# Convolution and attention kernel on one Trainium2 core: row maxima spread over the attention block, and two of its sixteen subtractions per block moved to GpSimd

## The chip, the core and the metric

The kernel runs on one core of a Trainium2 chip. Its engines are TensorE (PE, with its weight loads shown as PEld), VectorE (DVE), ScalarE (ACT), GpSimd (POOL) and SyncE (SP, which only issues transfers here). Each runs its own list of instructions in order and waits on counting semaphores. The metric is the device time of one execution in microseconds, lower is better.

## The reference, cut to what matters

```python
# x: (8, 192, 64, 64).  Layer 0: attention inside each image, 4096 positions, 192 channels
xn = _gn(x)                                   # group norm, 32 groups
q  = prelu(conv1x1(xn, w1, b1), a1)           # 24 channels
k  = prelu(conv1x1(xn, w2, b2), a2)           # 24 channels
v  = prelu(conv1x1(xn, wa, ba), aa)           # 192 channels
score = softmax(einsum('bnc,bcm->bnm', q, k), axis=2)
x  = x + einsum('bnm,bmc->bnc', score, v)     # transposed back to (b, c, h, w)
# Layer 1: a per-channel chain of small (1, 3, 3, 3, 1) maps with tanh gates, at x-0.5 and x+0.5
lower, upper = logits(_gn(x) - 0.5), logits(_gn(x) + 0.5)
s = -sign(lower + upper)
x = x + maximum(abs(sigmoid(s * upper) - sigmoid(s * lower)), 1e-6)
```

## The kernel before

The eight images are worked one after another. For each there is a `phase_a` (projections q, k, v of this image, interleaved with layer 1 of the image before) and a `phase_b` (the attention). This change touches `phase_b` alone.

`phase_b` has 8 **blocks** j of 512 query columns. A block has 16 **pairs** p, each of two times 128 keys. For a pair, PE makes the scores (`scores`, 2 products of 512 columns, L1261) two pairs ahead; ACT takes the exponential twice, once to fp16 (`e_hi`, L732) and once to fp32 (`e_32`, L735, semaphore `full_ready`); DVE makes the **lower part** `e_lo = e_32 - e_hi` (`low`, L1058, 128x1024, semaphore `lo_ready`); and PE multiplies both halves with v in 8 groups of 3 products (L1486, L1488, L1490) into the block's own two PSUM banks. `e_32` has two buffers, so ACT's fp32 pass of pair q waits for the lower part of pair q-2.

The softmax needs the row maxima of the *next* block before its scores. In block j PE therefore also makes 32 **max tiles** for block j+1 (`max_tile`, L1438, one product of 128x512 each) in the two free PSUM banks, and DVE reduces each to one column (`reduce`, L1164, semaphore `max_red`). Tile m waits until reduction m-2 is done. `max_tiles(p, first)` says which tiles belong to pair p: in block 0 four per pair from pair 3, in the others three per pair from pair 0; `spots` says after which of the 8 groups they stand. After the last one DVE runs `split_max` (6 small steps, L1006 to L1011), PE transposes the result (`turn_max`, L1240, before pair 12), DVE copies it out (`rows_out`, L1018) and SP carries it into `qst`.

At a block's start DVE takes the reciprocal of the row sums of the block before (`denominators`, L1025), ACT scales its output (`normalise`, 4 passes, L722, semaphore `out_norm`), POOL splits it (`split_out`, L688 and L690), PE turns it back in two halves (`turn_parts`, L1253, at the ends of pairs 12 and 13) and DVE adds x and takes statistics (`add_half`, L1033 and L1035). The free banks are those of the block before, so the first max tiles wait for `out_norm`.

Beside this run the **tails** of layer 1 of the image before: two units per block in blocks 0 to 5, and none during image 0. A unit is `sums` and `difference` on POOL (L582, L588, L593), `halves` and `size` on ACT, `result` on DVE (L1053, in pairs 7 and 15). ACT's `halves` stand in pairs 2 and 9, and POOL's L588 waits for them. DVE's order inside a pair p is: (p = 0: `denominators`), `low` of pair p+1, the reductions of pair p, then `result`.

Of the kernel before, what the change touches and what calls it, by code (L numbers as in the profile page):

```python
# [5 lines left out]
ALU = mybir.AluOpType  # L6
# [18 lines left out]
LN2 = 0.6931471805599453  # L25
ESHIFT = 14 * LN2
BIG = 4096.0
PER_STEP = 3
START = 1


# [82 lines left out]
    return USES[n - 1] if n == len(USES) - 1 else USES[n - 3] if n >= 3 else None  # L114


def max_tiles(p, first):

    per, begin = (4, 3) if first else (PER_STEP, 0)
    return list(range(max(per * (p - begin), 0), min(max(per * (p - begin + 1), 0), MAXES)))  # L120


def tail_unit(i, last):
# [26 lines left out]
def program(nc, x, wall, cols, g6, sel, eye, diag, mraw, fraw, braw, x2d, out):  # L150
    x_rows = x.rearrange("b c h w -> (b c) (h w)")
    out_rows = out.rearrange("b c h w -> (b c) (h w)")
    with ExitStack() as ctx:
# [348 lines left out]
        def _(pool):  # L502
# [155 lines left out]
            def moments(b, which):  # L658
# [17 lines left out]
                else:  # L676
                    step(pool.tensor_scalar(mv_next[:, :, 0], minus_mean1[:, :], -1.0, None, ALU.mult))
                    step(pool.tensor_scalar(mv_next[:, :, 1], total1[:, :], 1.0 / HW, None, ALU.mult))

            def split_out(b, j):  # L680

                normalised = pool.compute_val(b * BLOCKS + j + 1 + START)
                turned = pool.compute_val(b * 2 * BLOCKS + 2 * j + START)
                cast = pool.compute_val(b * (BLOCKS - 1) + j + 1)
                settle(pool)
                pool.wait_ge(out_norm, normalised)
                pool.wait_ge(out_turn, turned)
                pool.tensor_copy(o_parts[:, 0, :, :], o_sb[:, :, :]).then_inc(out_hi, 1)  # L688
                pool.wait_ge(out_hi, cast)
                pool.tensor_tensor(o_parts[:, 1, :, :], o_sb[:, :, :], o_parts[:, 0, :, :], ALU.subtract  # L690
                                   ).then_inc(out_split, 1)

            def phase_b(b, l):
                for j in range(BLOCKS):
                    if j == 4:
                        moments(b, 0)
                    if j == BLOCKS - 1:
                        moments(b, 1)
                    if j >= 1:
                        split_out(b, j - 1)  # L700
                    if l is not None:
                        for i in tails_in(j, HALVES_AT).values():
                            sums(l, i, False)
                            difference(l, i, False)
                root1(pool.compute_val(b + 1))

            root1(None)
# [9 lines left out]
        def _(act):  # L717
# [9 lines left out]
            def exps(pairs, q):  # L727
                sc = ps[:, 2 * (q % 2):2 * (q % 2) + 2, :]
                act.wait_ge(scored, pairs + (q + 1))
                if q >= 4:  # L730
                    act.wait_ge(summed, pairs + (q - 3))
                act.activation(e_hi[:, q % 4, :].rearrange("p (k n) -> p k n", k=2), sc, ACT.Exp)  # L732
                if q >= 2:
                    act.wait_ge(lo_ready, pairs + (q - 1))
                act.activation(e_32[:, q % 2, :].rearrange("p (k n) -> p k n", k=2), sc,  # L735
                               ACT.Exp).then_inc(full_ready, 1)

# [89 lines left out]
            def phase_b(b, l):  # L827
# [21 lines left out]
                for j in range(BLOCKS):  # L849
                    pairs = act.compute_val(b * BLOCKS * PAIRS)  # L850
                    for p in range(PAIRS):
                        if p == 0 and j > 0:
                            normalise(b, j - 1)
                        if p + 2 < PAIRS or j + 1 < BLOCKS:
                            exps(pairs, j * PAIRS + p + 2)
# [18 lines left out]
        def _(dve):  # L874
# [286 lines left out]
            def phase_b(b, l):  # L1161
                def reduce(base, m, bank):
                    dve.wait_ge(max_mm, base + (m + 1))
                    dve.tensor_reduce(mxp[:, m // BLOCKS, m % BLOCKS:m % BLOCKS + 1], ps[:, bank + m % 2, :],  # L1164
                                      AX_X, ALU.max).then_inc(max_red, 1)

                for j in range(BLOCKS):
# [6 lines left out]
                    for p in range(PAIRS):  # L1174
                        if p == 0 and not first:
                            denominators(b, j - 1)
                        if p == 12 and not last:
                            rows_out(nxt, free, False)
                        if p + 1 < PAIRS or not last:
                            low(pairs, p + 1)  # L1180
                        if first and l is not None and p == 1:
                            logits(l, UNITS - 1, False)
                        if not last:
                            for m in max_tiles(p, first):
                                reduce(maxes, m, free)
                            if p == 11:
                                split_max(nxt, maxes)
                        if not first and p in (13, 14):
                            add_half(b, j - 1, p - 13)
                        if l is not None and p in tails_in(j, RESULT_AT):  # L1190
                            result(l, tails_in(j, RESULT_AT)[p], False)
                        if last and p == 2:
# [17 lines left out]
        def _(pe):  # L1210
# [220 lines left out]

            def phase_b(b, l):
                def max_tile(base, q_col, m, bank, evacuated):
                    if m >= 2:
                        pe.wait_ge(max_red, base + (m - 1))
                    elif evacuated is not None:
                        pe.wait_ge(out_norm, evacuated + START)
                    pe.matmul(ps[:, bank + m % 2, :], qst[:, q_col + m // BLOCKS * P:q_col + (m // BLOCKS + 1) * P],  # L1438
                              kst[:, (m % BLOCKS) * N:(m % BLOCKS + 1) * N], start=True, stop=True
                              ).then_inc(max_mm, 1)  # L1440

                for j in range(BLOCKS):
# [6 lines left out]
                    for p in range(PAIRS):  # L1449
                        if p == 12 and not last:  # L1450
                            turn_max(blocks + 1, free)
                        if p + 2 < PAIRS or not last:
# [4 lines left out]
                        pe.wait_ge(lo_ready, pairs + (p + 1))  # L1457
# [38 lines left out]
                        if not first and p in (12, 13):  # L1496
                            if p == 12:
                                pe.wait_ge(out_split, b * (BLOCKS - 1) + j)
                            elif not last:
                                pe.wait_ge(max_rows, blocks + 2)  # L1500
                            turn_parts(j - 1, p - 12)

                pe.wait_ge(full_ready, pairs + PAIRS)
                project(0)
# [71 lines left out]
```

## Time and profile before

| | |
|---|---|
| median of 3 runs | 4865.89 us (4865.57 to 4873.28) |
| profiled execution | 4868.1 us, its span 4866.3 us |
| granted TensorE clock, mean of the span | 0.982 |
| busy share | PE 92%, DVE 86%, ACT 76%, POOL 19% |
| chain that ended last | PE 57%, DVE 17%, issue 13%, ACT 12% |
| reductions of max tiles in `phase_b` (L1164) | 1792, mean 683 ns |
| lower parts (L1058) | 1024, mean 1316 ns |

A row of the timeline gives start, duration, engine, line, operation, what is written from what, and how many instructions were merged in the row; in brackets how long the engine sat idle before it, and who ended that. Successive instructions of an engine overlap a little, so the distance from start to start is shorter than the duration. A busy share is an average over phases with different limits.

### The profile page before, as it was taken

What the parts mean: (1) busy time and instruction counts of PE and PEld (TensorE: products, weight loads), DVE (VectorE), ACT (ScalarE), POOL (GpSimd) and SP (SyncE); (2) the same over time, 40 slices, a digit from 0 to 9 for tenths busy, and PEclk for the clock granted to TensorE, in tenths of its full rate; (3) what the DMA queues carried; (4) which work ended last, traced back from release to release, by engine and by line L of the source; (5) the groups of instructions that cost most, each with busy time, mean ns of one, the idle gap of its engine ahead of it and who ended that gap; (6) DMA issues with size and microseconds to landing.
All of it is one profiled execution on the core that took longest, in us unless ns stands there. A gap on an engine that the chain in (4) does not pass through costs nothing.

```text
span 4866.3 us, 107519 instructions
## 1 busy us (share of the span) xinstructions
PE 4460.5 (92%) x38780; PEld 2978.2 (61%) x38780; DVE 4178.8 (86%) x5433; ACT 3717.8 (76%) x4214; POOL 937.5 (19%) x937
## 2 busy tenths in 40 slices
PE   6999989999899998999899998999989999899976
PEld 4888347773477725777257762678617785277821
DVE  6897899978999798996999969899698987989866
ACT  2776887768877697776977769777797777977787
POOL 4200202212122111221112120121202212022112
PEclk9999999999999999999999999999999999999988
DMA  2001421114211142111412023120332113311133
GB/s 66 25 20 30 100 70 47 34 39 105 62 47 40 36 110 51 47 40 46 108 45 57 28 62 98 39 58 27 77 86 60 36 38 73 96 42 34 38 88 95
DMA packets 154989, 279.95 MB, mean 58 GB/s; under 512 B 37441, under 2 KB 37921, under 8 KB 152706
## 3 DMA queue, kind: packets, MB, share of 16 engines
q1 hardware_dynamic: 154434, 272.69, 21.8%
q8 instruction: 331, 5.42, 0.5%
q14 instruction: 224, 1.84, 0.1%
HBM read 205.24 MB, written 50.33 MB: 53 GB/s over the span
## 4 chain that ended last, share of the span: by engine, by line
PE 57%; DVE 17%; issue 13%; ACT 12%; DMA 1%; DVEq 0%; ACTq 0%; SPq 0%; POOL 0%; POOLq 0%
PE ps L1486 10%; PE ps L1488 10%; PE ps L1490 10%; PE ps L1261 7%; DVE mxp L1164 6%; PE ps L1438 6%; ACT th L777 5%; ACT arena L770 5%; DVE arena L1058 4%; PE ps L1360 3%; PE ps L1294 3%; DVE th L1096 3%; PE ps L1346 3%; PE ps L1318 2%; PE ps L1253 1%
## 5 line engine op out<-in xcount | busy, mean ns | idle before, releaser
L1486 PE MATMUL ps<-v_sb,arena 128*128 128x193 f16 x8192 | 2017.5, 246 | 18.4 <-DVE arena L1058 18.4
L1488 PE MATMUL ps<-v_sb,arena 128*128 128x192 f16 x8192 | 2026.6, 247 | 0.0
L1490 PE MATMUL ps<-v_sb,arena 128*128 128x193 f16 x8192 | 2009.6, 245 | 0.0
L732 ACT ACTIVATE arena<-ps 128x1024 f16<-128x1024 f32 x1024 | 1049.9, 1025 | 773.8 <-PE ps L1261 772.8
L1058 DVE TENSOR_TENSOR arena<-arena 128x1024 f16<-128x1024 f32 x1024 | 1346.1, 1316 | 258.4 <-ACT arena L735 258.3
L1164 DVE TENSOR_REDUCE mxp<-ps 128x1 f32<-128x512 f32 x1792 | 1162.2, 683 | 32.5 <-PE ps L1438 24.8
L1096 DVE SCALAR_TENSOR_TENSOR th<-th,gates,ps 128x1024 f32<-128x1024 f32 x768 | 949.9, 1275 | 148.7 <-ACT th L777 141.4
L735 ACT ACTIVATE arena<-ps 128x1024 f32<-128x1024 f32 x1024 | 1046.4, 1022 | 0.2 <-DVE arena L1058 0.2
L1488 PEld LDWEIGHTS ps<-v_sb,arena 128*128 128x128 f16 x8192 | 794.8, 97 | 261.8 <-issue 0.3
L777 ACT ACTIVATE th<-ps,biases 128x1024 f32<-128x1024 f32 x768 | 826.1, 1120 | 119.9 <-PE ps L1346 81.5
L1486 PEld LDWEIGHTS ps<-v_sb,arena 128*128 128x128 f16 x8192 | 792.0, 97 | 150.5 <-issue 28.6
L1490 PEld LDWEIGHTS ps<-v_sb,arena 128*128 128x128 f16 x8192 | 807.2, 99 | 0.2
L1438 PE MATMUL ps<-kst,qst 128*128 128x512 f16 x1792 | 680.3, 380 | 56.1 <-DVE mxp L1164 49.7
L1261 PE MATMUL ps<-qst,kst 128*128 128x512 f16 x2048 | 612.5, 381 | 12.3 <-DMA qst<-mrows 8.5
L1360 PE MATMUL ps<-th,w 64*64 64x512 f32 x3072 | 421.4, 617 | 112.1 <-DVE th L1096 107.6
L770 ACT ACTIVATE arena<-x,biases,scl 128x1024 f32<-128x1024 f32 (+1 forms) x400 | 499.6, 1249 | 16.2 <-DVE biases L986 15.5
L1346 PE MATMUL ps<-arena,w1s 64*64 64x512 f32 x3072 | 426.6, 624 | 39.3 <-DMA arena<-x2d 8.3
L1346 PEld LDWEIGHTS ps<-arena,w1s 64*64 64x64 f32 x3072 | 90.8, 133 | 313.0 <-issue 292.6
L1360 PEld LDWEIGHTS ps<-th,w 64*64 64x64 f32 x3072 | 95.7, 133 | 280.0 <-issue 279.8
L1438 PEld LDWEIGHTS ps<-kst,qst 128*128 128x128 f16 x1792 | 172.4, 96 | 112.0 <-DVE mxp L1164 103.9
L1261 PEld LDWEIGHTS ps<-qst,kst 128*128 128x128 f16 x2048 | 184.7, 97 | 88.3 <-DMA qst<-mrows 14.9
L758 ACT ACTIVATE lu<-ps 128x384 f32<-128x384 f32 (+1 forms) x192 | 102.8, 536 | 170.6 <-PE ps L1269 117.1
(147 smaller groups left out, 3448.3 us busy)
## 6 DMA issues: line engine op xcount, KB each, us to landing
x<-x2d SPq DMA_DIRECT2D x1152, 64.0 KB, 2.4
arena<-x2d SPq DMA_DIRECT2D x768, 64.0 KB, 2.5
xp<-x_dram SPq DMA_DIRECT2D x18, 1536.0 KB, 10.1
shared<-x_dram SPq DMA_DIRECT2D x64, 384.0 KB, 3.7
x2d<-shared SPq DMA_DIRECT2D x64, 384.0 KB, 3.0
res<-x2d SPq DMA_DIRECT2D x96, 256.0 KB
out_dram<-res SPq DMA_DIRECT2D x96, 256.0 KB
kst<-shared SPq DMA_DIRECT2D x32, 256.0 KB, 3.3
```

The costliest lines, as they stand in the source:

```text
L732: act.activation(e_hi[:, q % 4, :].rearrange("p (k n) -> p k n", k=2), sc, ACT.Exp)
L735: act.activation(e_32[:, q % 2, :].rearrange("p (k n) -> p k n", k=2), sc, ACT.Exp).then_inc(full_ready, 1)
L770: ins = act.activation(t0[lo:hi, v % T0R, d, :], x4[lo:hi, v % X4R, :], ACT.Tanh, bias=biases[lo:hi, d, 0, u:u + 1], scale=scl[lo:hi, u:u ...
L777: act.activation(dst, ps[:, at:at + 2, :], ACT.Tanh, bias=biases[:, d, layer, u:u + 1]).then_inc(after, 1)
L1058: dve.tensor_tensor(e_lo[:, q % 4, :], e_32[:, q % 2, :], e_hi[:, q % 4, :], ALU.subtract).then_inc(lo_ready, 1)
L1096: dve.scalar_tensor_tensor(t, t, gates[:, c // 4, col:col + 1], ps[:, at:at + 2, :], ALU.mult, ALU.add).then_inc(after, 1)
L1164: dve.tensor_reduce(mxp[:, m // BLOCKS, m % BLOCKS:m % BLOCKS + 1], ps[:, bank + m % 2, :], AX_X, ALU.max).then_inc(max_red, 1)
L1261: ins = pe.matmul(ps[:, 2 * (q % 2) + i, :], kst[:, m * P:(m + 1) * P], qst[:, q_col:q_col + N], start=True, stop=True)
L1438: pe.matmul(ps[:, bank + m % 2, :], qst[:, q_col + m // BLOCKS * P:q_col + (m // BLOCKS + 1) * P], kst[:, (m % BLOCKS) * N:(m % BLOCKS + 1 ...
L1486: pe.matmul(acc, eh, v_sb[:, m, 0:C + 1], start=(m == 0 and t % 2 == 0), stop=False, skip_group_check=True)
L1488: pe.matmul(acc[:, 0:C], eh, v_sb[:, m, VW:VW + C], start=False, stop=False, skip_group_check=True)
L1490: ins = pe.matmul(acc, el, v_sb[:, m, 0:C + 1], start=False, stop=(m == MT - 1), skip_group_check=True)
```

## The change

The 32 max tiles of a block are laid out anew. Five of them (tiles 0 to 4) are made, and reduced, one block earlier, in its pairs 13, 14 and 15 (`EARLY_AT`: one, two and two tiles), where blocks 1 to 7 had none; the other 27 stand in pairs 0 to 10 as 2, 3, 2, 3, ... (`PER_PAIR`). The early ones exist for the maxima of blocks 2 to 7 (`j + 2 < BLOCKS`, so they are made in blocks 0 to 5). The two banks of the tiles swap. Because early tiles are in the banks in which the next block adds up, PE waits at pair 0 for `max_red` to reach the fifth of them; the wait for `out_norm` now stands before tiles 5 and 6. `turn_parts` and `add_half` move up one pair. In blocks 0 to 6 the lower parts of pairs 7 and 8 are made by POOL, counted on `lo_pool`, and POOL's `sums` and `difference` of the block's second unit come behind them.

```diff
+POOL_LOWS = (7, 8)
+EARLY_AT = {13: [0], 14: [1, 2], 15: [3, 4]}
+EARLY = 5
+PER_PAIR = [2, 3, 2, 3, 2, 3, 2, 3, 2, 3, 2]
...
 def max_tiles(p, first):
-    per, begin = (4, 3) if first else (PER_STEP, 0)
-    return list(range(max(per * (p - begin), 0), min(max(per * (p - begin + 1), 0), MAXES)))
+    if first:
+        return list(range(max(4 * (p - 3), 0), min(max(4 * (p - 2), 0), MAXES)))
+    begin = EARLY + sum(PER_PAIR[:p])
+    return list(range(begin, begin + PER_PAIR[p])) if p < len(PER_PAIR) else []
...
+def early_tiles(j, p):
+    return EARLY_AT.get(p, []) if j + 2 < BLOCKS else []
...  # GpSimd
+            def low(b, q):
+                full = pool.compute_val(b * BLOCKS * PAIRS + q + 1)
+                settle(pool)
+                pool.wait_ge(full_ready, full)
+                pool.tensor_tensor(e_lo[:, q % 4, :], e_32[:, q % 2, :], e_hi[:, q % 4, :], ALU.subtract
+                                   ).then_inc(lo_pool, 1)
...  # ScalarE, exps
                 if q >= 2:
-                    act.wait_ge(lo_ready, pairs + (q - 1))
+                    made, count = lower_part(b, q - 2)
+                    act.wait_ge(made, count)
...  # VectorE
-                        if p + 1 < PAIRS or not last:
+                        if (p + 1 < PAIRS or not last) and not by_pool(j * PAIRS + p + 1):
                             low(pairs, p + 1)
...
-                        if not first and p in (13, 14):
-                            add_half(b, j - 1, p - 13)
+                        if not first and p in (12, 13):
+                            add_half(b, j - 1, p - 12)
+                        for m in early_tiles(j, p):
+                            reduce(dve.compute_val(maxes + MAXES), m, free)
...  # TensorE
                     if m >= 2:
                         pe.wait_ge(max_red, base + (m - 1))
-                    elif evacuated is not None:
+                    if evacuated is not None and m in (EARLY, EARLY + 1):
                         pe.wait_ge(out_norm, evacuated + START)
...
                         if p == 0 and not first:
                             pe.wait_ge(x2_ready, b * 2 * BLOCKS + 2 * (j - 1) + START)
+                            if not last:
+                                pe.wait_ge(max_red, maxes + EARLY)
...
-                        spots = (1, 3, 5, 7) if first else (5, 6, 7) if p == 0 else (2, 5, 7)
+                        spots = (1, 3, 5, 7) if first else (5, 7) if p == 0 else (2, 5, 7) if len(todo) == 3 else (3, 7)
+                        ahead = early_tiles(j, p).copy()
...
+                                if i * NT + t in ((6,) if p == 13 else (4, 7)) and ahead:
+                                    if ahead[0] < 2 and first:
+                                        pe.wait_ge(max_rows, blocks + 2)
+                                    elif ahead[0] < 2:
+                                        pe.wait_ge(x2_ready, b * 2 * BLOCKS + 2 * (j - 1) + ahead[0] + 1 + START)
+                                    max_tile(pe.compute_val(maxes + MAXES), q_next + N, ahead.pop(0), free, None)
```

On DVE, at the end of pair 15 of a block and the start of the next, before (`low`, the unit's `result`, and the reciprocal that opens the next block, then `low` and the first reductions):

```order
L1058 TENSOR_TENSOR arena<-arena 128x1024
L1053 SCALAR_TENSOR_TENSOR res<-lu,res 128x512
L1169 ISA
L1025 RECIPROCAL rden<-ps 128x4
L1057 REGISTER_ALU
L1058 TENSOR_TENSOR arena<-arena 128x1024
```

and now, at the same place:

```order
L1099 TENSOR_TENSOR arena<-arena 128x1024
L1204 REGISTER_ALU
L1205 TENSOR_REDUCE mxp<-ps 128x1
L1204 REGISTER_ALU
L1205 TENSOR_REDUCE mxp<-ps 128x1
L1094 SCALAR_TENSOR_TENSOR res<-lu,res 128x512
L1210 ISA
L1066 RECIPROCAL rden<-ps 128x4
L1098 REGISTER_ALU
L1099 TENSOR_TENSOR arena<-arena 128x1024
```

Two early reductions now stand between the lower part and the `result`, and so also ahead of the reciprocal.

On POOL, one block with two units, before (`split_out`, then `sums` and `difference` of both units):

```order
L688 CAST o_parts<-o_sb 128x768
L690 TENSOR_TENSOR o_parts<-o_sb,o_parts 128x768
L582 TENSOR_TENSOR lu_sign<-lu 128x512
L588 TENSOR_TENSOR lu<-lu 128x512
L593 TENSOR_TENSOR lu<-lu,lu_sign 128x512
L582 TENSOR_TENSOR lu_sign<-lu 128x512
L588 TENSOR_TENSOR lu<-lu 128x512
L593 TENSOR_TENSOR lu<-lu,lu_sign 128x512
```

and now:

```order
L722 CAST o_parts<-o_sb 128x768
L724 TENSOR_TENSOR o_parts<-o_sb,o_parts 128x768
L609 TENSOR_TENSOR lu_sign<-lu 128x512
L615 TENSOR_TENSOR lu<-lu 128x512
L620 TENSOR_TENSOR lu<-lu,lu_sign 128x512
L708 REGISTER_ALU
L711 TENSOR_TENSOR arena<-arena 128x1024
L708 REGISTER_ALU
L711 TENSOR_TENSOR arena<-arena 128x1024
L609 TENSOR_TENSOR lu_sign<-lu 128x512
L615 TENSOR_TENSOR lu<-lu 128x512
L620 TENSOR_TENSOR lu<-lu,lu_sign 128x512
```

The two lower parts (L711) stand between the two units.

On PE, at the end of pair 11, before (the last group, the transpose of the maxima, the scores of pair 14):

```order
L1486 MATMUL ps<-v_sb,arena 128x193
L1488 MATMUL ps<-v_sb,arena 128x192
L1490 MATMUL ps<-v_sb,arena 128x193
L1240 MATMUL ps<-eye,mparts 12x128
L1261 MATMUL ps<-qst,kst 128x512 x2
```

and now:

```order
L1534 MATMUL ps<-v_sb,arena 128x193
L1536 MATMUL ps<-v_sb,arena 128x192
L1538 MATMUL ps<-v_sb,arena 128x193
L1296 MATMUL ps<-eye,o_parts 96x128 x8
L1283 MATMUL ps<-eye,mparts 12x128
L1304 MATMUL ps<-qst,kst 128x512 x2
```

The first `turn_parts` (L1296) has come ahead of the transpose of the maxima (L1283).

## Rows read from the trace of the kernel before

**Rows 1.** The page's first line.

```profile
span 4866.3 us, 107519 instructions
```

**Rows 2.** The view of waits: engine, tile, line <- releaser: us, times, longest us.

```profile
PE ps L1438 <- DVE mxp L1164: 49.7, 141, 0.8
```

**Rows 3.** Timeline of DVE, image 2, block 3 with two units.

```profile
1427.07 0.18 DVE L1025 RECIPROCAL rden<-ps 128x4 f32<-128x4 f32 x1 [0.64 <-PE ps L1490]
...
1429.22 1.89 DVE L1164 TENSOR_REDUCE mxp<-ps 128x1 f32<-128x512 f32 x3 [0.55 <-PE ps L1438]
1431.02 1.44 DVE L1058 TENSOR_TENSOR arena<-arena 128x1024 f16<-128x1024 f32 x1
1432.39 1.87 DVE L1164 TENSOR_REDUCE mxp<-ps 128x1 f32<-128x512 f32 x3
...
1437.25 2.05 DVE L1058 TENSOR_TENSOR arena<-arena 128x1024 f16<-128x1024 f32 x1
1439.21 1.87 DVE L1164 TENSOR_REDUCE mxp<-ps 128x1 f32<-128x512 f32 x3
...
1463.61 1.21 DVE L1058 TENSOR_TENSOR arena<-arena 128x1024 f16<-128x1024 f32 x1
1464.74 0.17 DVE L1006 TENSOR_REDUCE mx<-mxp 128x4 f32<-128x32 f32 x1
...
1475.64 0.68 DVE L1053 SCALAR_TENSOR_TENSOR res<-lu,res 128x512 f32<-128x512 f32 x1
1476.97 0.18 DVE L1025 RECIPROCAL rden<-ps 128x4 f32<-128x4 f32 x1 [0.65 <-PE ps L1490]
```

**Rows 4.** Timeline of ACT, the same block.

```profile
1427.36 1.36 ACT L722 ACTIVATE o_sb<-ps,rden 128x192 f32<-128x192 f32 x4
1428.59 1.04 ACT L732 ACTIVATE arena<-ps 128x1024 f16<-128x1024 f32 x1
...
1433.98 1.02 ACT L732 ACTIVATE arena<-ps 128x1024 f16<-128x1024 f32 x1 [1.22 <-PE ps L1261]
```

**Rows 5.** Timeline of POOL, the same block.

```profile
1429.74 1.64 POOL L690 TENSOR_TENSOR o_parts<-o_sb,o_parts 128x768 f16<-128x768 f32 x1
...
1436.94 1.27 POOL L588 TENSOR_TENSOR lu<-lu 128x512 f32<-128x512 f32 x1 [3.35 <-ACT lu L742]
1438.38 2.03 POOL L593 TENSOR_TENSOR lu<-lu,lu_sign 128x512 f32<-128x512 f32 x1 [0.17 <-POOL lu L588]
```

**Rows 6.** Timeline of PE, the same block.

```profile
1426.78 0.25 PE L1490 MATMUL ps<-v_sb,arena 128*128 128x193 f16 x1
1426.87 0.59 PE L1261 MATMUL ps<-qst,kst 128*128 128x512 f16 x2
1427.30 0.25 PE L1486 MATMUL ps<-v_sb,arena 128*128 128x193 f16 x1
...
1428.80 0.38 PE L1438 MATMUL ps<-kst,qst 128*128 128x512 f16 x1
...
1439.95 0.39 PE L1438 MATMUL ps<-kst,qst 128*128 128x512 f16 x1 [0.48 <-DVE mxp L1164]
1440.17 0.59 PE L1261 MATMUL ps<-qst,kst 128*128 128x512 f16 x2
...
1465.97 0.22 PE L1240 MATMUL ps<-eye,mparts 128*12 128x128 f16 x1 [0.87 <-DVE mparts L1011]
...
1468.57 0.61 PE L1253 MATMUL ps<-eye,o_parts 128*96 128x128 f16 x8
```

**Rows 7.** Timelines of POOL and DVE where both start almost together.

```profile
156.15 1.01 POOL L565 TENSOR_TENSOR w<-th 128x192 f32<-128x192 f32 x2
...
156.66 1.58 DVE L1058 TENSOR_TENSOR arena<-arena 128x1024 f16<-128x1024 f32 x1
...
694.11 2.35 POOL L582 TENSOR_TENSOR lu_sign<-xp 128x512 f32<-128x512 f32 x1
694.12 1.22 DVE L1058 TENSOR_TENSOR arena<-arena 128x1024 f16<-128x1024 f32 x1
```

More of the change, by code:

```diff
@@ L27 @@
 BIG = 4096.0
-PER_STEP = 3
+POOL_LOWS = (7, 8)
+EARLY_AT = {13: [0], 14: [1, 2], 15: [3, 4]}
+EARLY = 5
+PER_PAIR = [2, 3, 2, 3, 2, 3, 2, 3, 2, 3, 2]
 START = 1
@@ L114, in tile_user, with by_pool, lows_of @@
     return USES[n - 1] if n == len(USES) - 1 else USES[n - 3] if n >= 3 else None
+def by_pool(q):
+    return q // PAIRS + 1 < BLOCKS and q % PAIRS in POOL_LOWS
+def lows_of(pool, n):
+    return sum(by_pool(q) == pool for q in range(n))
 def max_tiles(p, first):
-    per, begin = (4, 3) if first else (PER_STEP, 0)
-    return list(range(max(per * (p - begin), 0), min(max(per * (p - begin + 1), 0), MAXES)))
+    if first:
[4 more added lines that the diff above has]
+    return EARLY_AT.get(p, []) if j + 2 < BLOCKS else []
 def tail_unit(i, last):
@@ L296, in program @@
         lo_ready = sem("lo_ready")
+        lo_pool = sem("lo_pool")
         summed = sem("summed")
@@ L330, in settle, with lower_part @@
             eng.wait_ge(consts_in, CONST_DMAS * 16)
+        def lower_part(b, q):
+            pool = by_pool(q)
+            return lo_pool if pool else lo_ready, b * lows_of(pool, BLOCKS * PAIRS) + lows_of(pool, q + 1)
         def counter(l):
@@ L700, in phase_b @@
                         split_out(b, j - 1)
[L701 to L704, printed above, removed]
+                    now = tails_in(j, HALVES_AT) if l is not None else {}
+                    for q in POOL_LOWS:
+                        if q == POOL_LOWS[0] and HALVES_AT[0] in now:
+                            sums(l, now[HALVES_AT[0]], False)
+                            difference(l, now[HALVES_AT[0]], False)
+                        if by_pool(j * PAIRS + q):
+                            low(b, j * PAIRS + q)
+                    if HALVES_AT[1] in now:
+                        sums(l, now[HALVES_AT[1]], False)
+                        difference(l, now[HALVES_AT[1]], False)
                 root1(pool.compute_val(b + 1))
@@ L725, in normalise, with exps @@
                 ins.then_inc(out_norm, 1)
-            def exps(pairs, q):
+            def exps(pairs, q, b=None):
                 sc = ps[:, 2 * (q % 2):2 * (q % 2) + 2, :]
@@ L854, in phase_b @@
                         if p + 2 < PAIRS or j + 1 < BLOCKS:
-                            exps(pairs, j * PAIRS + p + 2)
+                            exps(pairs, j * PAIRS + p + 2, b)
                         if l is not None:
@@ L1163, in reduce @@
                     dve.wait_ge(max_mm, base + (m + 1))
-                    dve.tensor_reduce(mxp[:, m // BLOCKS, m % BLOCKS:m % BLOCKS + 1], ps[:, bank + m % 2, :],
+                    dve.tensor_reduce(mxp[:, m // BLOCKS, m % BLOCKS:m % BLOCKS + 1], ps[:, bank + (m + 1) % 2, :],
                                       AX_X, ALU.max).then_inc(max_red, 1)
@@ L1435, in max_tile @@
                         pe.wait_ge(max_red, base + (m - 1))
-                    elif evacuated is not None:
+                    if evacuated is not None and m in (EARLY, EARLY + 1):
                         pe.wait_ge(out_norm, evacuated + START)
-                    pe.matmul(ps[:, bank + m % 2, :], qst[:, q_col + m // BLOCKS * P:q_col + (m // BLOCKS + 1) * P],
+                    pe.matmul(ps[:, bank + (m + 1) % 2, :], qst[:, q_col + m // BLOCKS * P:q_col + (m // BLOCKS + 1) * P],
                               kst[:, (m % BLOCKS) * N:(m % BLOCKS + 1) * N], start=True, stop=True
@@ L1456, in phase_b @@
                             scores(q_col if p + 2 < PAIRS else q_next, p + 2)
-                        pe.wait_ge(lo_ready, pairs + (p + 1))
+                        made, count = lower_part(b, j * PAIRS + p)
+                        pe.wait_ge(made, count)
                         if p == 0 and first:
@@ L1495, in phase_b @@
                                     max_tile(maxes, q_next, todo.pop(0), free, None if first else blocks)
-                        if not first and p in (12, 13):
-                            if p == 12:
+                                if i * NT + t in ((6,) if p == 13 else (4, 7)) and ahead:
[4 more added lines that the diff above has]
+                                    max_tile(pe.compute_val(maxes + MAXES), q_next + N, ahead.pop(0), free, None)
+                        assert not todo and not ahead
+                        if not first and p in (11, 12):
+                            if p == 11:
                                 pe.wait_ge(out_split, b * (BLOCKS - 1) + j)
+                                if not last:
+                                    pe.wait_ge(max_red, maxes + MAXES)
                             elif not last:
                                 pe.wait_ge(max_rows, blocks + 2)
-                            turn_parts(j - 1, p - 12)
+                            turn_parts(j - 1, p - 11)
                 pe.wait_ge(full_ready, pairs + PAIRS)
```

## The prediction

> **What bounds the kernel now.** I read the page first: PE 92% and DVE 86% of the span [rows 1] say only that two engines are close. Then the view of waits: PE stands for a reduction of a max tile 141 times [rows 2]; its weight loads wait likewise. So where PE waits inside the attention, it is for DVE's reductions, which stand behind `low` in DVE's list. Then the timelines of one block with two units: from reciprocal to reciprocal it takes 1476.97 - 1427.07 = 49.90 us [rows 3]. There are 35 such blocks (blocks 1 to 5 of seven images).
>
> PE's own work in it, from starts to starts [rows 6]: 18 products in 1428.80 - 1427.30 = 1.50, so 24 in 2.00 and a group of three in 0.25; the scores 0.44; a max tile 0.22 (512 columns; 0.215 below); a `turn_parts` 0.61 less the 0.17 by which an end outlasts its start, 0.44; `turn_max` 0.15. Sum: 16 x 2.44 + 32 x 0.215 + 0.88 + 0.15 = 46.9. **So PE stands 3.0 us per such block.** DVE's list is nearly as long: a lower part is followed after 1.13 (1463.61 to 1464.74), a reduction after 0.60 (three in 1.80) [rows 3].
>
> The 3.0 us, part by part: pair 0, 0.23 (its third tile needs the first reduction: 1428.80 + 0.42 + 0.68 + 0.06 = 1429.96 against 1429.73). Pair 1, 0.08 (first reduction at 1432.39). Before pair 12, 1.04 (0.87 idle for `split_max` [rows 6], and the 0.17 of the product's tail). The rest, 1.6 us, is DVE's backlog: in pairs 3 and 4 POOL's tail collides with `low` (2.05 instead of 1.21 [rows 3, 5]), 0.48 of one wait is seen before the tile at 1439.95 [rows 6], and in pair 8 it is the `result` of 0.60.
>
> **What the change does.** PE's products are the same in number. I replay one block with units; zero is the start of the last product of pair 15 (1426.78), every offset from the rows.
>
> *Moved: the early tiles.* The fifth follows that product at 0.08; its reduction starts 0.42 later (1428.80 to 1429.22 [rows 3, 6]), at 0.50, and is done at 1.18. Pair 0 would start at 0.52 + 0.22 = 0.74; the new wait holds it to 1.24 (0.06 from reduction to PE: 1439.21 + 0.68 to 1439.95). **Stall (a) 0.50**, before 0.
>
> *Added: what is queued behind that reduction.* On DVE the `result` (1.10, 0.60 long) and the reciprocal, now at 1.70 and not at 0.29. ACT's `normalise` starts 0.29 later, at 2.0, and lasts 1.36 [rows 3, 4]: `out_norm` at 3.36, where tile 5 is due at 1.24 + 1.50 = 2.74 and gets in at 3.43. **Stall (b) 0.69**, before 0.23. Without a unit the reciprocal is at 1.10, and (b) is 0.07.
>
> *What is late next.* Pair 1 starts at 3.43 + 0.22 + 0.50 + 0.22 + 0.44 = 4.81. POOL's L690 starts 2.38 after `normalise` (1429.74 - 1427.36), at 4.38, and ends at 6.02; ACT's first pass for pair 2 starts 1.23 after it, at 3.23, so its lower part is due at about 5.2 and finds POOL in its way. DVE is free for reductions 1.01 after L690's end (1431.38 to 1432.39 [rows 3, 5]), at 7.03; tile 7 is reduced at 7.71, tile 9 enters at 7.77 and was due at 4.81 + 2.43 = 7.24. **Stall (c) 0.53**, before 0.08; without a unit it is 0.55, by the same steps.
>
> *Pairs 3 and 4.* L588 starts 2.96 after ACT's pass for pair 4, and `low` 0.31 after L588 (1437.25 - 1436.94): blocked. Pair 2 now has two tiles, so `low` comes one tile, 0.22, sooner: 0.09 after L588. Who wins? A `low` 0.01 behind POOL's start took its plain 1.22 and POOL 2.35 (plain 1.27); where it was about 0.03 behind the second of two L565, it took 1.58 and ended 1.08 after them [rows 7]. So POOL wins from some 0.03 on, and 0.09 is on its side by 0.06 only. Then DVE is free 2.27 after L588's start (1439.21 - 1436.94); L588 starts 3.15 into pair 2 (the pass at 1433.98 starts 0.63 after its scores, these 0.44 before the pair; estimate from the 0.59 of the scores [rows 6]), the tile two after it enters at 3.15 + 2.27 + 0.68 + 0.06 = 6.16 and was due at 2.87 + 2.43 = 5.30. **Stall (d) 0.86**, before 1.2 (the rest above less pair 8); the fewer tiles after it hold no second one.
>
> The Trainium skill, "SBUF — State Buffer", section "SBUF: two separate sides", says that a DVE operation with two SBUF inputs and a GpSimd operation exclude each other for a whole instruction, and that the one that starts first gets the ports. The long rows agree (2.05, 2.35); the 0.01 case went to the later one. By the rule as by my threshold (d) stays; it speaks against giving POOL more such work.
>
> *Removed from DVE: two lower parts*, 2 x 1.13 = 2.3 us per block. They empty DVE in pairs 6 to 8 and cover the `result` of pair 7: **stall in pair 8 gone, 0.4**. Elsewhere PE does not wait for DVE's total, so the rest buys nothing. POOL's lower part is not in the trace: L690 is the same subtraction with 768 columns, 1.64, so 1.64 x 1024/768 = 2.19; bounds 1.64, and 2.19 + 1.08 = 3.3 when it must first let a `low` pass (694.11: 2.35 - 1.27). It is due some 4 us after `full_ready` (scores two pairs ahead, 5.9 before their products, less 0.6 and two passes of 1.0, gives 3.7 to 4.0), so it is hidden at either bound. ACT's pass of pair 9 waits for pair 7's later still. The unit behind them is needed by ACT in pair 9 and is ready in pair 8.
>
> *Moved: `turn_parts`* now fills the wait for `split_max`. The collision at `low` of pair 11 stays (three tiles in pair 9, as now): free at 5.42 of pair 9, two reductions, `low` at 6.62, `turn_max` 2.36 later (1463.61 to 1465.97) at 8.98; PE is ready at 3.08 + 2.87 + 2.00 + 0.44 = 8.39. **Stall (e) 0.59**, before 1.04. Without units: `low` 3.23 into pair 10, `turn_max` at 5.59, PE ready at 5.31, 0.28 against 0.22, since the last tile now stands later in its pair.
>
> **Sum.** With units: 0.50 + 0.69 + 0.53 + 0.86 + 0.59 = 3.17 against 3.0: +0.17 x 35 = +6. Image 0, blocks 1 to 5: 0.50 + 0.07 + 0.55 + 0.28 = 1.40 against 0.23 + 0.08 + 0.22 = 0.53: +0.87 x 5 = +4.4. Block 0 (8 of them): five tiles more on PE +1.08, stall (a) at its end +0.50, and in pairs 6 and 7, where four reductions and a `low` (4 x 0.62 + 1.13 = 3.6) outlast PE's 3.30, -0.64: +0.94 x 8 = +7.5. Block 6: five tiles fewer, -1.08, new stalls 1.50 (b, c, 0.28) or 0.90 in image 0, old ones 0.53: -0.11 x 7 - 0.7 = -1.5. Block 7 and `phase_a`: 0. Total +16 us. The profiled execution (4868.1) lies 2.2 above the median; I apply the sum to the median: **4882 us**.
>
> **Rivals.** (1) *DVE wins in pair 3.* It needs `low` 0.06 earlier or L588 later; then (d) is gone, the block takes 49.2, and the sum is 16 - 0.86 x 35 = -14: 4852. For it: the small margin; against: both offsets repeat from block to block. (2) *The boundary stalls do not come*, because the early reductions are done before PE asks. Then the block falls to PE's own 46.9 and (e), 47.5: 2.4 x 35 = 84 less, block 0 +4: 4786. For it: DVE loses 2.3 us of work; against: the fifth tile is PE's last product before the wait. (3) *POOL's pair is later than I think*: if the two lower parts together come 1.0 later, the unit behind them (L582, 1.27) meets DVE's `low` of pair 9 and holds PE some 0.9 in 42 blocks: +38, 4920. Below that point nothing. (4) *Part of each*: the stalls hide behind one another and the sum stays within 0.2%, about what a measurement of this kernel can tell: 4866.
>
> **How the numbers follow.** Forecast 0.50, (1) 0.16, (2) 0.08, (3) 0.09, (4) 0.17. The forecast's own range is 4873 to 4896 (0.2 us per block in blocks 1 to 6 is 8 us). Leaving out (2) and the far half of (3) the range is 4848 to 4905. Faster by over 0.2% has (1) and (2), 0.24; within 0.2% has (4) and a tail of the forecast, 0.21; slower has the rest, 0.55.
>
> **What would show it.** PE's first product of a block waiting for a reduction (some 48 times 0.5), tile 5 waiting for ACT's `normalise` 42 times 0.7, the reciprocal at 1.7 us after the block's last product, `low` of pair 4 at 2.2 us and no stall in pair 8, POOL's L711 at about 2.2 us. Wrong it would be if `low` of pair 4 takes 1.2 us, if L711 takes over 3.5, or if pair 0 starts without a wait.

## The result, and the profile after

| | before | after |
|---|---|---|
| median | 4867.85 us, 4 runs (4865.57 to 4873.28) | 4914.1 us, 4 runs (4911.66 to 4914.45) |
| ratio | 1 | 1.0091, 95% interval 1.0078 to 1.0104 |
| span of the profiled execution | 4866.3 us | 4912.6 us |

One execution of all that are told of here, one of e9, took 5893 us at a granted clock of 0.725 (the others have 0.97 to 0.99) and enters no figure. The change makes the kernel slower, by 46 us where 16 were forecast: the time lies above the range. The page of the changed kernel, its first line and the engines, and from its list of groups (busy us, mean ns | idle before, releaser) three rows:

```profile
span 4912.6 us, 109567 instructions
...
PE 4461.2 (91%) x38780; PEld 2978.7 (61%) x38780; DVE 4078.4 (83%) x5321; ACT 3709.6 (76%) x4214; POOL 1161.4 (24%) x1049
...
L1534 PE MATMUL ps<-v_sb,arena 128*128 128x193 f16 x8192 | 2020.1, 247 | 61.5 <-POOL arena L711 25.5
...
L1205 DVE TENSOR_REDUCE mxp<-ps 128x1 f32<-128x512 f32 x1792 | 1196.8, 686 | 314.3 <-PE ps L1482 304.7
L1099 DVE TENSOR_TENSOR arena<-arena 128x1024 f16<-128x1024 f32 x912 | 1212.2, 1331 | 151.3 <-ACT arena L776 149.5
```

Against [rows 1] the span is 46.3 longer, and DVE is busy for less of it, 83% and not 86%: it lost 112 lower parts, and the kernel gained none of that time. The first group has the news: the products stood 25.5 us for POOL's L711. The view of one line says how often:

```profile
L711 POOL TENSOR_TENSOR arena<-arena x112: 2124/2127/2137, 146.7 to 4622.9; 128x1024 f16<-128x1024 f32 x112
...
  PE ps L1534: 25.5, 1
  ACT arena L776: 24.4, 1
```

Of 112 lower parts by POOL (2.13 us each, estimate 2.19) one pair held everybody, once, for 25.5 us. The first of them starts at 146.7. This is the timeline of POOL, and of PE, in block 0 of image 0:

```profile
98.05 1.26 POOL L551 TENSOR_TENSOR th<-th 128x12 f32<-128x12 f32 x1 [17.69 <-DVE th L951]
...
142.55 0.22 POOL L589 TENSOR_TENSOR th<-th 128x12 f32<-128x12 f32 x1
142.85 3.91 POOL L592 TENSOR_TENSOR w<-th 128x192 f32<-128x192 f32 x8
146.71 4.21 POOL L711 TENSOR_TENSOR arena<-arena 128x1024 f16<-128x1024 f32 x2
```

```profile
122.83 0.59 PE L1304 MATMUL ps<-qst,kst 128*128 128x512 f16 x2
148.89 0.34 PE L1534 MATMUL ps<-v_sb,arena 128*128 128x193 f16 x1 [25.47 <-POOL arena L711]
```

POOL is still working through its set-up: over a hundred steps on 12 columns, each waiting for the one before, from 98 to 143 us, and eight of 128x192 behind them, to 147. Before the change nobody wanted POOL in that block. Now PE asks for the lower part of pair 7 at 123 and gets it at 148.9. The clock fell while PE stood: granted 1.00 over 123 to 124, 0.90 over 124 to 126, 0.50 (1.2 GHz) over 126 to 151, and 1.00 again from 153. So the first products after the gap start 0.16 apart where they start 0.08 apart at the full clock; by an estimate, half of the 4 us from 149 to 153, that is 2 us more.

The length of each block, from the start of its first product to that of the next block's, read from the rows of PE for all 56:

| | before | after | forecast of the difference | difference |
|---|---|---|---|---|
| image 0, block 0 | 51.36 | 80.49 | +0.94 | +29.1 |
| images 1 to 7, block 0 (mean) | 52.67 | 53.85 | +0.94 | +1.18 |
| images 1 to 7, blocks 1 to 5 | 49.92 | 50.24 | +0.17 | +0.32 |
| image 0, blocks 1 to 5 (no units; mean) | 47.60 | 48.32 | +0.87 | +0.73 |
| block 6, images 1 to 7 | 47.52 | 47.38 | -0.11 | -0.14 |

Image 0's block 6, not in the table, went from 47.52 to 46.61, forecast -0.7. One block of 56 gives 29.1 of the 46.3. The view of waits of PE in the changed kernel, which answers to [rows 2]:

```profile
PE ps L1482 <- DVE mxp L1205: 53.4, 114, 0.8
...
PE ps L1482 <- ACT o_sb L762: 20.2, 42, 0.5
...
PE ps L1534 <- DVE mxp L1205: 17.6, 48, 0.4
```

The two lower rows are new, and they are the forecast's stalls (b), 42 times, and (a), 48 times (an idle row is 0.17 shorter than the delay, since an instruction's end outlasts the next one's start). The timelines of DVE and POOL in image 2, block 3, beside [rows 3, 5]:

```profile
1464.20 0.68 DVE L1094 SCALAR_TENSOR_TENSOR res<-x,res 128x512 f32<-128x512 f32 x1
1464.80 0.18 DVE L1066 RECIPROCAL rden<-ps 128x4 f32<-128x4 f32 x1
...
1474.76 2.26 DVE L1099 TENSOR_TENSOR arena<-arena 128x1024 f16<-128x1024 f32 x1
...
1490.62 0.68 DVE L1094 SCALAR_TENSOR_TENSOR res<-lu,res 128x512 f32<-128x512 f32 x1
1491.22 1.22 DVE L1099 TENSOR_TENSOR arena<-arena 128x1024 f16<-128x1024 f32 x1
```

```profile
1474.67 1.27 POOL L615 TENSOR_TENSOR lu<-lu 128x512 f32<-128x512 f32 x1 [3.35 <-ACT lu L783]
```

The block's first product starts at 1464.34 and the reciprocal that opens it only at 1464.80, behind the `result`; the lower part of pair 4 comes 0.09 after POOL's L615 and takes 2.26 instead of 1.21. Both are as the prediction has them.

### The profile page after: what moved, and what is told of

It reads as the page before. It is cut to its first block, busy times and chain, and to the rows that moved or that the text cites. A ratio compares the mean times of both kernels' runs of the same rounds, so it can differ in the third digit from the quotient of the medians.

```text
span 4912.6 us, 109567 instructions
## 1 busy us (share of the span) xinstructions
PE 4461.2 (91%) x38780; PEld 2978.7 (61%) x38780; DVE 4078.4 (83%) x5321; ACT 3709.6 (76%) x4214; POOL 1161.4 (24%) x1049
## 4 chain that ended last, share of the span: by engine, by line
PE 52%; DVE 16%; issue 14%; ACT 13%; DMA 1%; DVEq 1%; SPq 0%; ACTq 0%; POOL 0%; POOLq 0%
PE ps L1534 9%; PE ps L1536 9%; PE ps L1538 9%; PE ps L1304 6%; PE ps L1482 5%; DVE mxp L1205 5%; ACT th L818 5%; ACT arena L811 4%; DVE arena L1099 4%; PE ps L1403 4%; PE ps L1337 3%; PE ps L1389 3%; DVE th L1137 3%; PE ps L1361 2%; DVE res L1094 1%
## 5 line engine op out<-in xcount | busy, mean ns | idle before, releaser
L1534 PE MATMUL ps<-v_sb,arena 128*128 128x193 f16 x8192 | 2020.1, 247 | 61.5 <-POOL arena L711 25.5
L1205 DVE TENSOR_REDUCE mxp<-ps 128x1 f32<-128x512 f32 x1792 | 1196.8, 686 | 314.3 <-PE ps L1482 304.7
L1099 DVE TENSOR_TENSOR arena<-arena 128x1024 f16<-128x1024 f32 x912 | 1212.2, 1331 | 151.3 <-ACT arena L776 149.5
L711 POOL TENSOR_TENSOR arena<-arena 128x1024 f16<-128x1024 f32 x112 | 238.3, 2128 | 457.8 <-ACT arena L776 457.8
L722 POOL CAST o_parts<-o_sb 128x768 f16<-128x768 f32 x56 | 46.1, 823 | 912.0 <-ACT o_sb L762 881.7
```

Of the source, the lines that this page charges most:

```text
L1099: dve.tensor_tensor(e_lo[:, q % 4, :], e_32[:, q % 2, :], e_hi[:, q % 4, :], ALU.subtract).then_inc(lo_ready, 1)
L1534: pe.matmul(acc, eh, v_sb[:, m, 0:C + 1], start=(m == 0 and t % 2 == 0), stop=False, skip_group_check=True)
```

## The experiments

Line numbers of the experiments differ from those of the changed kernel by up to 6. Each ratio is against the kernel before as timed beside that run (medians 4867.99 us for e1 to e4, 4873.63 for e5 to e8, 4869.47 for e9 to e12), so between these three groups ratios compare and times do not quite. "Step of pair n" is from the first product of a pair to that of the next, as a mean over blocks 1 to 5 of images 1 to 7.

**e1_block0_by_dve**: the changed kernel, but in image 0, block 0, VectorE makes all lower parts.

```diff
-                        if by_pool(j * PAIRS + q):
+                        if by_pool(j * PAIRS + q) and not (l is None and j == 0):
...  # VectorE
+                        elif first and l is None and by_pool(p + 1):
+                            low(pairs, p + 1, lo_pool)
```

> The change, but in block 0 of image 0 the two lower parts stay with DVE, which counts them on lo_pool. Theory S (the part that was missed is GpSimd's set-up chain, behind which those two lower parts stood until 146.7 us; everything else is as the sum has it): block 0 of image 0 falls from 80.5 to about 52.3 us, the span from 4912.6 to about 4884.5, still some 17 us above the kernel before; no other block moves. Theory B (the lower part on GpSimd is late in general and block 0 is only where it shows first): other waits for GpSimd's lower part appear, and less than 15 of the 46 us come back, over 4897.

4886.44 us, ratio 1.0043 (1.0029 to 1.0057). Block 0 of image 0 takes 52.14 us; the other blocks are as in the changed kernel. So the 28 us are these two instructions' and no more. With them out the time stands 4 us from the forecast of 4882, which is closer than the sum deserves: in the profiled executions the 56 blocks together are 20.4 us longer than before, and what lies outside them 3.6 shorter.

**e2_lows_alone** and **e3_tiles_alone**: e1's kernel with the tiles, `turn_parts` and `add_half` of before, so that only POOL's lower parts are left of the change; and the changed kernel with all lower parts on VectorE, so that only the rest is.

```diff
-EARLY_AT = {13: [0], 14: [1, 2], 15: [3, 4]}
-EARLY = 5
-PER_PAIR = [2, 3, 2, 3, 2, 3, 2, 3, 2, 3, 2]
+EARLY_AT = {}
+EARLY = 0
+PER_PAIR = [3] * 10 + [2]
...  # e3
-POOL_LOWS = (7, 8)
+POOL_LOWS = ()
```

> The max tiles, turn_parts and add_half as in the kernel before; only the two lower parts per block on GpSimd (not in block 0 of image 0), with the second unit behind them. Theory R (PE waits only at single places, which the hand replay names): in blocks 1 to 5 of seven images the 0.43 before pair 9 and the 0.52 of pair 4 go (the second unit's L582 no longer meets the lower part of pair 5), the turn_max wait stays: 48.95 instead of 49.92; block 0 0.65 less. Sum -33 - 5 = -38, span 4828, ratio 0.992. Theory L (DVE's load bounds these blocks): 2.3 us in each of 56 blocks, down to PE's own time in most, -80 or more, under 4790.

> The tiles, turn_parts and add_half of the change; all lower parts on DVE, GpSimd's two units one behind the other as before. Theory R: nothing that GpSimd's lower parts bought is needed once the tiles are spread, but block 0 keeps its 0.65: span 4884.5 + 5 = 4890, blocks 1 to 5 50.2 as in the change. Theory L: 2.3 us more DVE work in each block costs time: blocks 1 to 5 over 51.5, span over 4930.

e2: 4855.33 us, 0.9976 (0.9966 to 0.9986), and not 4828. The change's lower parts alone, with POOL's second unit behind them, are worth 12 us: blocks 1 to 5 take 49.45 against 49.92, and all of it is at pair 4, whose step falls from 3.61 to 3.09 as the expectation has it. These are POOL and DVE of before there, and DVE of e2:

```profile
1440.55 1.27 POOL L582 TENSOR_TENSOR lu_sign<-lu 128x512 f32<-128x512 f32 x1
...
1441.01 1.89 DVE L1058 TENSOR_TENSOR arena<-arena 128x1024 f16<-128x1024 f32 x1
```

```profile
1439.51 1.21 DVE L1099 TENSOR_TENSOR arena<-arena 128x1024 f16<-128x1024 f32 x1
```

In e2 POOL starts that operation only after its two lower parts. So what the steps show is a collision put off, and not a relief of VectorE; the second unit put later without the lower parts was not tried. The stall of pair 8 did not go: its step stays at 3.51 against the 3.09 of its neighbours with three tiles. DVE's timeline there:

```profile
1450.49 1.41 DVE L1205 TENSOR_REDUCE mxp<-ps 128x1 f32<-128x512 f32 x2 [0.28 <-PE ps L1484]
1451.82 0.68 DVE L1094 SCALAR_TENSOR_TENSOR res<-lu,res 128x512 f32<-128x512 f32 x1
1452.41 1.22 DVE L1099 TENSOR_TENSOR arena<-arena 128x1024 f16<-128x1024 f32 x1
1453.55 1.88 DVE L1205 TENSOR_REDUCE mxp<-ps 128x1 f32<-128x512 f32 x3
```

DVE was idle just before (0.28), so it carries no backlog that fewer lower parts could empty; `result` and `low` stand back to back ahead of three reductions, and PE asks for the first while they run. Two tiles in pair 8 cure that (e3's step is 2.87), and so does a `result` that stands elsewhere (e12, below). e3: 4886.95 us, 1.0041 (1.0027 to 1.0055), within its interval of e1. **With the tiles of the change POOL's lower parts are worth nothing.**

**e4_result_earlier**: e1 with the second unit's `result` in pair 14, so that the reciprocal of the next block is behind one thing less.

```diff
-HALVES_AT, SIZE_AT, RESULT_AT = (2, 9), (5, 12), (7, 15)
+HALVES_AT, SIZE_AT, RESULT_AT = (2, 9), (5, 12), (7, 14)
```

> e1 with the second unit's result on DVE in pair 14 and not in pair 15, so that it no longer stands between the last early reduction and the reciprocal. Theory R: the wait for out_norm in pair 0 falls from 0.67 to 0.07 in 42 blocks, -26, span 4858. Rival (pair 0 and 1 wait for something else that comes at the same time, as GpSimd's split of the output): under 10 us come back, over 4874.

4864.63 us, 0.9998 (0.9988 to 1.0007): 22 us less than e1, where 26 were expected. The step of pair 0 falls from 3.54 to 2.93. Stall (b) was the `result` ahead of the reciprocal.

**e6_pair2_tile**: e4 with the second of pair 2's tiles one group of products earlier. It is to put VectorE's `low` of pair 4 ahead of POOL's L615; the number of tiles in each pair stays.

```diff
-... (2, 5, 7) if len(todo) == 3 else (3, 7)
+... (2, 5, 7) if len(todo) == 3 else (3, 6) if p == 2 else (3, 7)
```

> e4 with the second tile of pair 2 after the seventh group and not after the eighth, 0.25 us sooner, so that DVE asks for the lower part of pair 4 some 0.17 us before GpSimd starts L588 of the first unit. Theory R (who starts first has the ports): this lower part takes 1.2 instead of 2.26, wait (d) of 0.86 goes in 35 blocks, -30, span 4831, and GpSimd's L588 takes 2.3 instead of 1.27. Rival (DVE is short of time there anyway): the wait moves one pair on, under 10 us come back.

4837.15 us, 0.9928 (0.9911 to 0.9945). The step of pair 3 falls from 3.95 to 3.08, the block of image 2 from 49.61 to 48.75: stall (d), 0.86, is the collision. POOL and DVE of e6:

```profile
1438.48 2.18 POOL L615 TENSOR_TENSOR lu<-lu 128x512 f32<-128x512 f32 x1 [3.36 <-ACT lu L783]
...
1438.32 1.22 DVE L1099 TENSOR_TENSOR arena<-arena 128x1024 f16<-128x1024 f32 x1
```

`low` now starts 0.16 before POOL instead of 0.09 after, takes its plain 1.22, and it is POOL that takes 2.18.

**e5_four_early**: e4 with four early tiles and not five, the last of them after the fifth group of pair 15, and pair 6 with three instead; pairs 1 and 2 change places.

```diff
-EARLY_AT = {13: [0], 14: [1, 2], 15: [3, 4]}
-EARLY = 5
-PER_PAIR = [2, 3, 2, 3, 2, 3, 2, 3, 2, 3, 2]
+EARLY_AT = {13: [0], 14: [1, 2], 15: [3]}
+EARLY = 4
+PER_PAIR = [2, 2, 3, 3, 2, 3, 3, 3, 2, 3, 2]
```

> e4 with four early tiles instead of five, so that PE's last product of a block is no tile whose reduction it then waits for, and with two tiles in pair 1 and three in pairs 2 and 6. Theory R: wait (a) of 0.50 goes in 48 blocks (-24); the third tile of pair 1, whose wait (c) of 0.55 comes from GpSimd's split meeting the lower part of pair 2, is gone (-26); (d) in pair 3 is 0.65 instead of 0.86 (-7). Span 4861.3 - 57 = 4805. Rival (the waits at the boundary are GpSimd's split and ACT's scaling, whatever the tiles do): they move to the next pair, less than 25 come back, over 4836.

4814.84 us, 0.9883 (0.9866 to 0.9899). The step of pair 15 falls from 3.45 to 2.85, that of pair 1 from 3.63 to 2.86, and pair 3 has 3.73 instead of 3.95. Less the tile (0.215) that pairs 15 and 1 each lost, stall (c) is gone and stall (a) falls from 0.58 to 0.20. It was expected to go altogether. DVE and PE of e5 at the end of a block:

```profile
1418.38 0.69 DVE L1205 TENSOR_REDUCE mxp<-ps 128x1 f32<-128x512 f32 x1
...
1419.12 0.26 PE L1536 MATMUL ps<-v_sb,arena 128*128 128x193 f16 x1
```

The fourth tile's reduction stands behind a `low` and is done at 1419.07, 0.05 before the next block's first product starts. So the new wait of the change still bounds the block's start, by less.

**e11_five_without_pool**: e5 with every lower part on VectorE (`POOL_LOWS = ()`).

> This is e5_four_early with every lower part made by VectorE. It asks what the lower parts on GpSimd are worth once the tiles stand well. Theory A (nothing: VectorE has room around pairs 6 to 8, as e3_tiles_alone equals e1_block0_by_dve within its interval): 4815, within 8. Theory B (they carry the gain of e5: VectorE gets 2 lows of 1.13 us more in pairs 6 to 8, where it idles about 1.0 us): up to 1.3 us more in a block, 35 blocks, 4860.

4809.27 us, 0.988 (0.9864 to 0.9897): the same as e5. Blocks 1 to 5 take 48.50 against 48.56. VectorE's two lower parts more fall in pairs 6 to 8, where it idled between the reductions (in e5, 0.28, 0.71 and 0.28 us in a row).

**e9_two_tiles_in_pair2** and **e10_pair9_too**: e5 with a tile moved from pair 2 to pair 4, and then also one from pair 9 to pair 8, both to bring a `low` ahead of POOL.

```diff
-PER_PAIR = [2, 2, 3, 3, 2, 3, 3, 3, 2, 3, 2]
+PER_PAIR = [2, 2, 2, 3, 3, 3, 3, 3, 2, 3, 2]
...  # e10
+PER_PAIR = [2, 2, 2, 3, 3, 3, 3, 3, 3, 2, 2]
```

> This is e5_four_early with one maximum moved from pair 2 to pair 4. In e5 VectorE's low of pair 4 starts at 1428.43 us, 0.35 after GpSimd's L615 at 1428.08, and takes 2.01 instead of 1.22; TensorE waits 0.65 at pair 3 in blocks 1 to 5. Theory (whoever starts first on the shared port wins, and a queue of maxima decides who that is): with two maxima in pair 2 the low starts some 0.6 earlier, ahead of GpSimd, takes 1.22, and the step of pair 3 falls from 3.73 to 3.1. 35 blocks by 0.65 is 23 us: 4792. Rival (the load on VectorE alone decides, the collision is only a sign of it): the maximum moved to pair 4 brings the wait with it, and the time stays at 4815.

> As e9_two_tiles_in_pair2, with one more maximum moved from pair 9 to pair 8. In e5 the low of pair 11 starts at 1450.20, 0.30 after GpSimd's L615 at 1449.90, takes 2.05, and pushes the low of pair 12 back: the step of pair 11 is 3.73 with 0.85 of waiting. Theory: with two maxima in pair 9 the low of pair 11 is ahead of GpSimd, pair 11's step falls towards 2.9 to 3.3; but pair 8 with three maxima behind the result tile waits 0.43, as in e2_lows_alone. Net -0.2 to -0.4 in 35 blocks: 7 to 14 us under e9, about 4782. Rival: the two cancel and the time is that of e9, 4792.

e9: 4823.59 us (median of three), 0.991 (0.989 to 0.993); e10: 4843.94 us, 0.995 (0.9933 to 0.9967). Both missed their theories, and neither is the rival's time. The intervals of e9 and e5 just overlap, but the steps say that e9 is the slower: blocks 1 to 5 take 48.77 against 48.56. POOL and DVE of e5, and then of e9:

```profile
1428.08 1.27 POOL L615 TENSOR_TENSOR lu<-lu 128x512 f32<-128x512 f32 x1 [2.58 <-ACT lu L783]
...
1428.43 2.01 DVE L1099 TENSOR_TENSOR arena<-arena 128x1024 f16<-128x1024 f32 x1
```

```profile
1430.66 1.27 POOL L615 TENSOR_TENSOR lu<-lu 128x512 f32<-128x512 f32 x1 [2.58 <-ACT lu L783]
...
1430.14 0.69 DVE L1205 TENSOR_REDUCE mxp<-ps 128x1 f32<-128x512 f32 x1 [0.26 <-PE ps L1484]
1430.75 2.26 DVE L1099 TENSOR_TENSOR arena<-arena 128x1024 f16<-128x1024 f32 x1
```

I had counted a reduction less, 0.6. But the pair's last tile still comes from PE at the end of the pair; DVE waits 0.26 for it, and `low` gains only 0.26: from 0.35 after POOL to 0.09 after. That is still after, and a nearer miss costs more, for `low` ends at the same distance from POOL's start in both (2.36 and 2.35 us) while it is wanted sooner: the step of pair 3 grows from 3.73 to 3.96. In e10 the same happens at pair 11 (0.30 after POOL becomes 0.08, the step 3.73 becomes 3.91), and pair 8 with three tiles stalls again. What decides is where the last tile before the `low` stands, as in e6, and not how many there are.

**e7_tail_moved**, **e8_tail_late** and **e12_tail_halves_back** start from e2: the tiles of before, and `turn_parts` and `add_half` one pair earlier as in the change. They differ in the pairs at which a unit's halves, size and result stand.

```diff
-HALVES_AT, SIZE_AT, RESULT_AT = (2, 9), (5, 12), (7, 15)
+HALVES_AT, SIZE_AT, RESULT_AT = (2, 10), (5, 12), (11, 15)   # e7
+HALVES_AT, SIZE_AT, RESULT_AT = (10, 12), (12, 14), (14, 15)  # e8
+HALVES_AT, SIZE_AT, RESULT_AT = (2, 9), (5, 12), (11, 15)    # e12
```

In e8 POOL's lower parts also stand ahead of both units, and the units' stores come one later.

> e2 (no early tiles) with the units' stages moved on ScalarE and VectorE: halves of the second unit in pair 10 and not 9, result of the first in pair 11 and not 7; and turn_parts and add_half one pair earlier as in the change. Theory R: of the waits left in e2's blocks 1 to 5, pair 8's 0.43 goes (the result stands in a pair without tiles), pair 11's collision of 0.85 goes (L588 comes after the lower part of pair 12), turn_parts covers 0.2: 49.40 to 47.9, 35 times, and 1.2 in block 0: -52 - 8 - 3 = -63, span 4790. Theory L (DVE's load): nothing is taken off DVE, so under 10 us.

> e7 with both units late in the block: halves in pairs 10 and 12, size in 12 and 14, result in 14 and 15, GpSimd's lower parts ahead of both units, and SyncE's stores one unit later so that the transfer of the maxima does not stand behind a result. Theory R: the collision at the lower part of pair 4 (0.66) goes too, -23 against e7: 4767. Rival: ScalarE waits for GpSimd in pair 12 (sum of the second unit) and exps come late; then over 4790.

e7: 4856.21 us, 0.9966 (0.9954 to 0.9979), where 4790 was expected; e8: 4935.55 us, 1.0127 (1.0111 to 1.0144), where 4767 was. The step of pair 11 is 4.72 in e7 and 5.91 in e8, against 3.70 in e2. (In e8 pairs 0 and 12 grew too, from 3.33 to 3.91 and from 2.89 to 3.53; why was not followed up.) POOL and DVE of e7, where PE waits for `mparts`, and then DVE of e12:

```profile
1460.35 1.93 POOL L615 TENSOR_TENSOR lu<-lu 128x512 f32<-128x512 f32 x1 [9.86 <-ACT lu L783]
1462.44 1.26 POOL L620 TENSOR_TENSOR lu<-lu,lu_sign 128x512 f32<-128x512 f32 x1 [0.17 <-POOL lu L615]
```

```profile
1461.06 0.18 DVE L1047 TENSOR_REDUCE mx<-mxp 128x4 f32<-128x32 f32 x1
1461.28 1.02 DVE L1048 TENSOR_SCALAR negm<-mx 128x4 f32<-128x4 f32 x1
1462.33 0.17 DVE L1049 TENSOR_SCALAR mparts<-negm 128x4 f16<-128x4 f32 x1
1462.54 1.19 DVE L1050 SCALAR_TENSOR_TENSOR rest<-mparts,negm 128x4 f32<-128x4 f16 x1
```

```profile
1454.20 0.17 DVE L1047 TENSOR_REDUCE mx<-mxp 128x4 f32<-128x32 f32 x1
1454.41 0.17 DVE L1048 TENSOR_SCALAR negm<-mx 128x4 f32<-128x4 f32 x1
...
1454.82 0.16 DVE L1050 SCALAR_TENSOR_TENSOR rest<-mparts,negm 128x4 f32<-128x4 f16 x1
```

With the halves a pair later POOL's two operations (plain 1.27 and 1.26) lie not beside `low` but beside `split_max`, steps on four columns that PE waits for one after the other. Two of them are held for a microsecond; in e8, where POOL has three such operations in a row, three are. That reading was put to the test:

> This is e7_tail_moved with GpSimd's second unit back at pair 9 from pair 10. In e7 GpSimd's L615 and L620 lay beside split_max, a chain of six VectorE steps of 0.17 us, and two of these took 1.02 and 1.19; TensorE waited for turn_max, 1.5 us at pair 11. Theory (the collision with the short steps is what ate e7's gain): the steps are back at 0.17 each (1.9 us less), the low of pair 11 or 12 takes 2.05 again (0.8 more), the step of pair 11 falls from 4.72 to about 3.7, 36 us in 35 blocks and a few in the other blocks: 4815 to 4825. Rival (turn_parts a pair earlier simply brings 0.6 us of products ahead of turn_max and does nothing else): 4856, as e2 and e7.

4811.94 us, 0.9885 (0.9868 to 0.9901). The steps are back at 0.17, the `low` of pair 11 takes 2.06 (2.05 in e2), and the step of pair 11 is 3.68. Blocks 1 to 5 take 48.56 against e2's 49.45: 0.42 from pair 8, out of which the `result` has gone, and 0.45 from pair 13, out of which half of `turn_parts` has gone. The theory held, and this kernel with the tiles of before is as fast as e5 and e11.

## Why the prediction was wrong

- **The step that failed** is the cover of POOL's lower part: "it is hidden at either bound", and with it "Block 0 (8 of them) ... +0.94 x 8". The cover was worked out in a steady block and carried to all 56. In image 0, block 0, POOL has its set-up to end: 29.1 us measured for 0.94. The rows for it were at hand, one of [rows 7] is POOL's L565 at 156.15, between its own set-up steps. e1 shows that these two instructions were the whole of what lay outside the range: without them 4886 us, inside it.
- **The replay of the steady block** held. Steps less PE's own work give (a) 0.51, (b) 0.67, (c) 0.56 and (d) 0.87 for 0.50, 0.69, 0.53 and 0.86; (e) is 0.61 for 0.59 by the rows (0.44 idle before the transpose and the 0.17), but 0.69 by pair 11's step. The block grew by 0.32 and not 0.17, 5 us in 35 blocks. e4 and e6 took (b) and (d) away, each by removing its named cause; e5 took (c) away and 0.38 of (a).
- **"They empty DVE in pairs 6 to 8 and cover the `result`"** had the right size, 0.4, and the wrong cause: it is the two tiles in place of three (e2 keeps the stall with POOL's lower parts, e3 loses it without).
- **Rival 3**, POOL's pair late, named the mechanism but put it at a unit behind it, a microsecond in 42 blocks; it came at the front, once, for 25. Rivals 1 and 2 did not come: `low` lost at 0.09, and PE waited 48 times for the fifth tile.
- That 4886 is only 4 from 4882 is in part luck. Outside the blocks 4.1 us came back (2081.0 to 2076.9 in the changed kernel), where the sum has 0. The stretches from the last pair of an image to the next image's first product went from 1450.6 to 1444.7 us in all. What of this is the change's and what differs from one execution to the next was not tried: single blocks 0 differ by 1.5 us within one execution of either kernel.

## What to carry to other kernels

Before an engine with little work gets something that others wait for, look at what it does the first time the block runs, and not in a steady block alone: a share of 24% busy says nothing of its first 150 us. Where two engines' operations hold each other up, as `low` and L615 do here, they are to be placed by starts, to a tenth of a microsecond, and the last wait ahead of it sets that start. A collision moved is not a collision removed: beside a long operation it cost 0.85, beside a chain of short ones 1.9. And work moved ahead of a boundary brings a wait at that boundary: PE's new wait for the last early reduction took 0.58 a block in e4, and 0.20 in e5, whose last early tile comes sooner. That is a third of e5's gain over e4 in blocks 1 to 5; half is pair 1's third tile, taken out of POOL's way.

## What the runs showed of the hardware

- Of two such operations the one that starts first runs at its plain time, and the other is held until it ends. VectorE's `low` (plain 1.22) started against GpSimd's L615 (plain 1.27): 0.16 before, 1.22, and GpSimd took 2.18 (e6); 0.09 after, 2.26 (e9); 0.35 after, 2.01 (e5). That fits the Trainium skill, "SBUF — State Buffer", section "SBUF: two separate sides", by which the one that starts first gets the shared pair of ports for the whole instruction. In all traces together, beside GpSimd's operations of 128x512, a `low` that started 0.08 or 0.09 after was held every time (245), and one that started 0.07 to 0.17 before never was (49). The exception is in the trace of before: seven times, one of them in [rows 7], GpSimd's L582 started 0.01 or less ahead of `low` and was yet the one held.
- Not only a long operation with two inputs is held: a TENSOR_SCALAR on 4 columns with one input took 1.02 instead of 0.17 (e7). The reductions of the max tiles, out of PSUM, never grew: 0.67 to 0.69 in every trace, beside GpSimd's L620 too.
- The best kernels here are e5, e11 and e12, 1.2% under before and within each other's intervals, by two different ways. e11 with two tiles in pair 2, the second one group earlier as in e6, was not tried, and neither was e12 without POOL's lower parts.
